# A two-layer transformer kernel: VectorE takes q's low part ahead of the two parts of the negated maxima

## The chip, the cores and the metric

The kernel runs on one core of one Trainium2 chip. The metric is the device time of one execution in microseconds (us), as the median of several runs. Engines are named as in the profile: PE is TensorE (its matrix multiplications; PEld its weight loads), DVE is VectorE, ACT is ScalarE, POOL is GpSimd, SP the queue that issues DMAs. L1232 is line 1232 of the kernel.

## The reference

The input x has 8 sequences of 512 rows of 128 values. Two layers follow one another, each an attention and a mixture of experts, with residuals:

```
x = x + cosine_attention(layernorm(x))         # 16 heads of 8, q and k normalized
x = x + top1_experts(layernorm(x))             # 8 experts, 128 -> 32 -> 128, gelu
x = x + causal_attention(layernorm(x))         # 16 heads of 64, softmax
x = layernorm(x + top2_experts(layernorm(x)))  # 8 experts, 128 -> 512 -> 128, gelu
```

The change touches the causal attention of the second layer. For each sequence and head it computes `a = q @ k.T / 8`, sets what lies above the diagonal to minus infinity, takes the softmax over the keys, multiplies by v, and projects all heads to 128 values. All is float32.

## The kernel before, in words

The 16 heads of the causal attention are taken in pairs, 8 pairs to a sequence, 64 in all. The main loop (`early_steps`) makes passes `i` over sequences and in each pass 8 steps `p` (0 to 7), one for each pair; every engine has its own program of the same loop, and semaphores alone connect them. The passes of this text are numbered by `i`; those from 0 to 7 have the causal attention of sequence `i`. A step works on several stages at once: scores and exponentials of pair g, the row maxima of pair g+1, the projections q and k of pair g+2, and the values of pair g-1. Beside them it carries a share of the work of other sequences: cosine attention (two batches of exponentials a step), layer norms, small experts, routing. After the passes comes the sparse second mixture of experts.

**High and low parts.** A projection lands in PSUM. ACT casts it to the matrix format fp32r (the high part, L941). DVE then subtracts the high part from the PSUM value (the low part, `lo_part`, L1209). The score is a sum of three products of such parts. The subtraction frees the PSUM bank that the projection lies in, and it waits for ACT's cast (`qk1_hi`). It occurs twice in a step, for q and for k.

**The maxima.** PE first computes scores from high parts alone (L1679), in three units to a pair. DVE adds the causal mask to them and reduces each row to its negated maximum (L1216, `maxima`). Then `maxima_parts` splits the 128x8 values into two bfloat16 parts with two operations on SBUF:

```
unit_done(dve, "max", g, 1)
unit_done(dve, "max", g, 2)
link(v.tensor_tensor(hl[:, :, :, 0], neg_max[:], neg_max[:], ALU.max))          # L1232
v.tensor_tensor(hl[:, :, :, 1], neg_max[:], hl[:, :, :, 0],
                ALU.subtract).then_inc(negmax_ready, 1)                         # L1233
```

`link` makes DVE wait until the first has completed. PE transposes the parts (L1690, `max_transposed`, the item "mT"), ACT moves them to SBUF, and the final scores of the next step take them in by a fourth product.

**What sets the order.** Each engine executes its program strictly in the order written. Two PSUM banks named `work` take all small results in turn; `work_order` lists the items of a step, and neighbours in that list lie in different banks, so that an item can be written only when the one two places before has been moved away. Around the change the list reads: q, one item that depends on the step, the row sums of pair g-1 ("sum", L1740 and L1742), mT, k. The item in between is a value projection in step 0, the transposed rows xtT, xh2T or xnT in steps 1 to 3, router logits in step 4 and the fourth q/k/v projection of the cosine attention in step 5; steps 6 and 7 have none, and in other steps it is missing where the sequence that it belongs to doesn't exist (the first and the last passes). PE's program has the same order: project q, the item, sums, mT, values of the cosine attention (L1856), project k, cosine scores (L1843).

**POOL's part.** When the sums are through PE, POOL may overwrite their operands: three additions over SBUF, one behind the other (L795 on 768 values a partition, L798 on 512, L801 on 256), each linked to the one before by a semaphore.

**DVE behind the change.** After q's low part DVE has, by step: the move of xh2T (step 2), of router logits (4), eight subtractions that split the operands of the cosine attention (L1251; steps 1, 3, 5, 7), four standardizations (L1185, step 5); then in every step the normalization by the inverse row sums (L1240), k's low part, and moves of transposed operands (L1262) that PE makes (L1829) when L1251 is done.

Of the kernel before, what the change touches and what calls it, by code (L numbers as in the profile page):

```python
# [281 lines left out]
def layers_kernel(nc, x, wqkv0, g_scale, wg0, s0, bias_ln0, w1_0, b1_0, w2_0, b2_0,  # L282
# [3 lines left out]
    with ctx:  # L286
# [280 lines left out]
        def work_bank(*name):  # L567
            return work[:, WORK_NO[name] % 2, :]
# [9 lines left out]
        def work_wait(eng, *name):  # L578

            eng.wait_ge(work_full[WORK_NO[name] % 2], work_fills(*name))  # L580
            return work_bank(*name)
# [8 lines left out]
        def free_of(*name):  # L590
            return work_free[WORK_NO[name] % 2]
# [15 lines left out]
        def unit_done(eng, *unit):  # L607
            eng.wait_ge(score_free[UNIT_NO[unit] % 2], unit_fills(*unit) + 1)
# [514 lines left out]
        def _(dve):  # L1123
# [3 lines left out]
            def link(ins):  # L1127

                links[0] += 1
                ins.then_inc(dve_step, 1)  # L1130
                dve.wait_ge(dve_step, links[0])
# [73 lines left out]
            def lo_part(which, hi, lo, g, n):  # L1205

                w = work_bank(which, g)
                dve.wait_ge(qk1_hi, n)
                v.tensor_tensor(lo[:, g % 2, :], w, hi[:, g % 2, :].bitcast(F32),  # L1209
                                ALU.subtract).then_inc(free_of(which, g), 1)  # L1210
# [8 lines left out]
            def maxima(g, i):  # L1219

                d = unit_wait(dve, "max", g, i)
                for j in range(2):
                    for qt, at in (((3, 0),), ((2, 0), (0, 3 * P)), ((1, 0),))[i]:
                        last = masked_max(d, qt, at, j)
                last.then_inc(unit_free("max", g, i), 1)

            def maxima_parts(g):

                unit_done(dve, "max", g, 1)
                unit_done(dve, "max", g, 2)  # L1230
                hl = neg_max_hl[:].rearrange("p t (j n) -> p t j n", j=2)
# [3 lines that stand above are left out]
# [192 lines left out]
            for o in early_steps():  # L1427
# [36 lines left out]
                    group_rows(s, p // 2 - 1)  # L1464
                if o.pair(1) is not None:
                    maxima(o.pair(1), 2)
                    maxima_parts(o.pair(1))
                if o.pair(2) is not None:
                    lo_part("q", q_hi, q_lo, o.pair(2), 2 * o.pair(2) + 1)
                if p == 2 and f is not None:  # L1470
                    w = work_wait(dve, "xh2T", f)
                    v.tensor_copy(xT_a, w).then_inc(free_of("xh2T", f), 1)
# [660 lines left out]
```

## Time and profile before

| | us |
|---|---|
| median of three runs | 1599.74 |
| lowest and highest | 1593.32, 1600.54 |
| the profiled execution | 1609.85 |
| its span on the core | 1608.1 |
| DVE busy | 979.8 (61%) |
| ACT busy | 863.5 (54%) |
| POOL busy | 605.1 (38%) |

Durations of single instructions come from the profiled execution, so sums are made against its time. A row of a timeline gives start, duration, engine, line and operation, the tiles written and read, their shapes and a count of merged instructions; what stands in square brackets is how long the engine had been idle before it and which instruction ended that. The granted clock of TensorE has two levels here, 1.00 (2.4 GHz) and 0.50 (1.2 GHz).

### The profile page before, as it was taken

What the parts mean: (1) busy time and instruction counts of PE and PEld (TensorE: products, weight loads), DVE (VectorE), ACT (ScalarE), POOL (GpSimd) and SP (SyncE); (2) the same over time, 40 slices, a digit from 0 to 9 for tenths busy, and PEclk for the clock granted to TensorE, in tenths of its full rate; (3) what the DMA queues carried; (4) which work ended last, traced back from release to release, by engine and by line L of the source; (5) the groups of instructions that cost most, each with busy time, mean ns of one, the idle gap of its engine ahead of it and who ended that gap; (6) DMA issues with size and microseconds to landing.
All of it is one profiled execution on the core that took longest, in us unless ns stands there. A gap on an engine that the chain in (4) does not pass through costs nothing.

```text
span 1608.1 us, 28398 instructions
## 1 busy us (share of the span) xinstructions
PE 1348.8 (84%) x9302; PEld 815.7 (51%) x9302; DVE 979.8 (61%) x3308; ACT 863.5 (54%) x1679; POOL 605.1 (38%) x783
## 2 busy tenths in 40 slices
PE   4778888889888888888888888989888987889873
PEld 1234444454545444544554545545555545778762
DVE  3565565656676666666666766565565653656664
ACT  4765555556555655565556555645433543455543
POOL 1000332233243324332433243325345445566564
PEclk7878899999999999999999999999899998999986
DMA  8050990000000000000000000001002001132412
GB/s 306 1 232 1 9 3 1 0 8 8 1 13 9 8 1 14 8 8 1 14 8 8 1 14 1 8 1 37 31 8 79 1 8 36 51 107 60 116 54 86
DMA packets 65455, 54.67 MB, mean 34 GB/s; under 512 B 41017, under 2 KB 51649, under 8 KB 65057
## 3 DMA queue, kind: packets, MB, share of 16 engines
q1 hardware_dynamic: 60768, 43.48, 12.6%
q0 software_dynamic: 4544, 9.38, 1.8%
q8 instruction: 79, 1.29, 0.3%
q14 instruction: 64, 0.52, 0.1%
HBM read 21.03 MB, written 31.81 MB: 33 GB/s over the span
## 4 chain that ended last, share of the span: by engine, by line
PE 62%; DVE 22%; ACT 11%; issue 3%; POOL 1%; DMA 0%; another core or an unknown queue 0%; SPq 0%; ACTq 0%; POOLq 0%; DVEq 0%
PE scores L1710 10%; PE work L1650 8%; PE outs L1856 7%; PE outs L1729 7%; DVE scores L1216 6%; ACT a_buf L935 6%; PE work L1759 4%; PE outs L2051 4%; PE scores L1679 4%; DVE ra L1209 3%; ACT ra L941 3%; DVE parts L1251 2%; PE scores L1843 2%; PE scores L2039 2%; PE work L1742 2%
## 5 line engine op out<-in xcount | busy, mean ns | idle before, releaser
L1216 DVE CUSTOM_DVE_ANT_0 scores<-scores,mask_qk 128x512 f32<-128x512 f32 (+3 forms) x512 | 239.1, 519 | 203.3 <-PE scores L1679 196.8
L785 POOL TENSOR_SCALAR_AFFINE_SELECT big<-big 128x256 f32<-128x256 f32 x256 | 101.6, 409 | 560.7 <-ACT big L929 560.4
L935 ACT ACTIVATE a_buf<-scores 128x1024 f32<-128x1024 f32 x256 | 248.2, 1028 | 104.7 <-PE scores L1843 104.4
L929 ACT ACTIVATE big<-scores 128x1024 f32<-128x1024 f32 (+1 forms) x192 | 169.4, 883 | 208.3 <-PE scores L1710 201.6
L1710 PE MATMUL scores<-ra 64*128 64x512 f32 (+3 forms) x1536 | 187.9, 350 | 37.6 <-ACT a_buf L935 24.3
L795 POOL TENSOR_TENSOR big<-big 128x768 f32<-128x768 f32 x64 | 117.0, 1828 | 151.3 <-PE work L1742 151.1
L1710 PEld LDWEIGHTS scores<-ra 64*128 64x128 f32 x1536 | 123.4, 191 | 88.2 <-ACT big L929 29.5
L1729 PE MATMUL outs<-big 128*64 128x512 f32 (+3 forms) x1024 | 162.4, 446 | 2.2 <-DVE yT L1240 2.2
L1856 PE MATMUL outs<-a_buf 128*16 128x512 f32 x1024 | 147.0, 650 | 1.5 <-ACT a_buf L935 1.4
L1090 ACT ACTIVATE big<-scores,b_sb 128x128 f32<-128x128 f32 x312 | 89.6, 371 | 83.3 <-PE scores L2039 46.9
L941 ACT CAST ra<-work 128x512 fp32r<-128x512 f32 x128 | 75.1, 586 | 96.5 <-PE work L1650 95.5
L1240 DVE TENSOR_TENSOR yT<-outs,rsum 128x512 f32<-128x512 f32 x64 | 44.1, 689 | 125.2 <-ACT rsum L952 125.2
L881 POOL DMA_INDIRECT choice_rows<-big x78 | 79.3, 1017 | 90.6 <-DVE big L1568 86.2
L1729 PEld LDWEIGHTS outs<-big 128*64 128x64 f32 x1024 | 64.6, 137 | 91.3 <-issue 78.1
L1209 DVE TENSOR_TENSOR ra<-work,ra 128x512 fp32r<-128x512 f32 x128 | 88.1, 689 | 33.5 <-ACT ra L941 28.4
L778 POOL TENSOR_TENSOR rstd<-var_eps,minus_half 128x4 f32<-128x4 f32 x48 | 50.2, 1046 | 149.4 <-DVE var_eps L1178 149.3
L1679 PE MATMUL scores<-ra 64*128 64x512 f32 (+3 forms) x512 | 82.8, 358 | 23.5 <-DVE neg_max L1216 20.0
L2051 PE MATMUL outs<-a_buf,big 128*128 x624 | 88.7, 288 | 8.2 <-ACT big L1090 3.7
L1843 PE MATMUL scores<-qkT 32*128 32x512 f32 x512 | 78.3, 515 | 17.6 <-ACT a_buf L935 12.6
L2051 PEld LDWEIGHTS outs<-a_buf,big 128*128 128x128 f32 x624 | 81.3, 203 | 9.9 <-issue 9.8
L1710 PE MATMUL scores<-neg_max_T,pick 64*128 64x512 f32 (+3 forms) x512 | 85.4, 328 | 0.0
L798 POOL TENSOR_TENSOR big<-big 128x512 f32<-128x512 f32 x64 | 82.4, 1287 | 5.0
(223 smaller groups left out, 2630.5 us busy)
## 6 DMA issues: line engine op xcount, KB each, us to landing
sorted_rows<-xrows SPq DMA_DIRECT2D x34, 520.0 KB, 6.7
big<-sorted_rows SPq DMA_DIRECT2D x78, 65.0 KB
a_buf<-in_w SPq DMA_DIRECT2D x2, 2048.0 KB, 8.2
a_buf<-in_x SPq DMA_DIRECT2D x8, 256.0 KB, 2.7
x_rows<-x SPq DMA_DIRECT2D x8, 256.0 KB, 2.0
ra<-x_rows SPq DMA_DIRECT2D x8, 256.0 KB
a_buf<-choice_rows SPq DMA_DIRECT2D x6, 256.0 KB, 3.8
yT<-choice_rows SPq DMA_DIRECT2D x5, 256.0 KB, 2.8
```

Of the source, the lines that this page charges most:

```text
L795: nc.gpsimd.tensor_tensor(tsum, prob1(g, 0)[:, :, P:SEQ], prob1(g, 1)[:, :, 0:3 * P], ALU.add).then_inc(tsum_step, 1)
L929: activation(prob1(g, i), d[:, :, 0:256] if i == 2 else d, ACT.Exp, scale=SCALE1).then_inc(unit_free("pair", g, i), 1)
L935: activation(prob0(c)[:, i * 1024:(i + 1) * 1024], unit_wait(act, "cosine", c, i), ACT.Exp).then_inc(unit_free("cosine", c, i), 1)
L941: copy(dst[:, g % 2, :], w).then_inc(qk1_hi, 1)
L1209: v.tensor_tensor(lo[:, g % 2, :], w, hi[:, g % 2, :].bitcast(F32), ALU.subtract).then_inc(free_of(which, g), 1)
L1216: return v.tensor_tensor_reduce(scores_, scores_, mask_qk[:, SEQ - width:SEQ], -1.0, 3e38, ALU.add, ALU.min, neg_max[:, qt, j:j + 1])
L1650: last = mm(dst, a, c, start=(n == 0), stop=(n == 2))
L1679: last = mm(d[:, j * SEQ + at:j * SEQ + at + width], q_hi[heads(j), g % 2, qt * P:(qt + 1) * P], k_hi[heads(j), g % 2, 0:width], start=(n ...
L1710: last = mm(d[:, j * SEQ + at:j * SEQ + at + width], lhs, c[heads(j), g % 2, queries], start=(n == 0 and term == 0), stop=(n == len(blocks ...
L1729: last = mm(outs[heads(j), 0, kb * P:], v1[:, kb, n * D1:(n + 1) * D1], probs, start=(kb == 0), stop=(kb == TILES - 1))
L1856: last = mm(outs[STRIP * j:STRIP * j + VCOLS, 1, :], vstat(s)[:, kb, g * HG + j, :], prob0(c)[:, j * SEQ:(j + 1) * SEQ], start=(kb == 0), ...
L2051: last = mm(y_bank, hid_T(n)[:, c * P:(c + 1) * P], w2_1_sb[:, bass.ds(expert[n] + c * P, DIM)], start=(c == 0), stop=(c == CH1 - 1))
```

## The change

In DVE's program of the main loop the call of `maxima_parts` goes behind that of `lo_part` for q. Both keep their conditions, and nothing else is altered.

```
@@ -1464,9 +1464,10 @@
                     group_rows(s, p // 2 - 1)
                 if o.pair(1) is not None:
                     maxima(o.pair(1), 2)
-                    maxima_parts(o.pair(1))
                 if o.pair(2) is not None:
                     lo_part("q", q_hi, q_lo, o.pair(2), 2 * o.pair(2) + 1)
+                if o.pair(1) is not None:
+                    maxima_parts(o.pair(1))
                 if p == 2 and f is not None:
                     w = work_wait(dve, "xh2T", f)
                     v.tensor_copy(xT_a, w).then_inc(free_of("xh2T", f), 1)
```

## Rows read from the trace of the kernel before

**Rows 1.** The page, parts 1 and 4: busy time, and the chain that ended last.
```profile
PE 1348.8 (84%) x9302; PEld 815.7 (51%) x9302; DVE 979.8 (61%) x3308; ACT 863.5 (54%) x1679; POOL 605.1 (38%) x783
PE 62%; DVE 22%; ACT 11%; issue 3%; POOL 1%; DMA 0%; another core or an unknown queue 0%; SPq 0%; ACTq 0%; POOLq 0%; DVEq 0%
```

**Rows 2.** List of waits: who waited for whom, us in total, times, longest.
```profile
PEld work L1740 <- DVE ra L1209: 44.0, 40, 1.4
...
PE work L1690 <- DVE ra L1209: 12.1, 20, 3.0
```

**Rows 3.** Timeline of an ordinary step (pass 4, step 0): start us, us, what.
```profile
805.23 0.59 ACT L941 CAST ra<-work 128x512 fp32r<-128x512 f32 x1 [0.83 <-PE work L1650]
...
805.55 0.20 DVE L1233 TENSOR_TENSOR neg_max_hl<-neg_max,neg_max_hl 128x8 bf16<-128x8 f32 x1
805.85 0.69 DVE L1209 TENSOR_TENSOR ra<-work,ra 128x512 fp32r<-128x512 f32 x1
...
807.61 0.40 PE L1690 MATMUL work<-ident_b,neg_max_hl 128*128 128x128 bf16 x4
...
807.77 1.83 POOL L795 TENSOR_TENSOR big<-big 128x768 f32<-128x768 f32 x1 [2.90 <-PE work L1742]
```

**Rows 4.** Timeline of a free step (pass 3, step 6).
```profile
767.98 0.20 DVE L1233 TENSOR_TENSOR neg_max_hl<-neg_max,neg_max_hl 128x8 bf16<-128x8 f32 x1
768.27 0.69 DVE L1209 TENSOR_TENSOR ra<-work,ra 128x512 fp32r<-128x512 f32 x1
...
768.73 1.82 POOL L795 TENSOR_TENSOR big<-big 128x768 f32<-128x768 f32 x1 [1.44 <-PE work L1742]
...
769.11 0.38 PE L1690 MATMUL work<-ident_b,neg_max_hl 128*128 128x128 bf16 x4 [0.48 <-DVE ra L1209]
...
770.63 1.28 POOL L798 TENSOR_TENSOR big<-big 128x512 f32<-128x512 f32 x1
```

**Rows 5.** Timeline of the first full step (pass 0, step 0).
```profile
169.33 1.82 POOL L795 TENSOR_TENSOR big<-big 128x768 f32<-128x768 f32 x1
...
169.69 1.52 DVE L1232 TENSOR_TENSOR neg_max_hl<-neg_max 128x8 bf16<-128x8 f32 x1
...
171.23 1.26 POOL L798 TENSOR_TENSOR big<-big 128x512 f32<-128x512 f32 x1
171.24 1.30 DVE L1233 TENSOR_TENSOR neg_max_hl<-neg_max,neg_max_hl 128x8 bf16<-128x8 f32 x1
...
173.27 0.38 PE L1690 MATMUL work<-ident_b,neg_max_hl 128*128 128x128 bf16 x4 [3.02 <-DVE ra L1209]
```

**Rows 6.** Instructions on the tile neg_max_hl: duration ns min/median/max, first and last start.
```profile
L1232 DVE TENSOR_TENSOR neg_max_hl<-neg_max x64: 194/196/1518, 153.3 to 1328.0; 128x8 bf16<-128x8 f32 x64
L1233 DVE TENSOR_TENSOR neg_max_hl<-neg_max,neg_max_hl x64: 194/196/1717, 153.5 to 1328.2; 128x8 bf16<-128x8 f32 x64
```

**Rows 7.** Timeline of a free step with operand parts (pass 3, step 7).
```profile
790.47 0.59 ACT L941 CAST ra<-work 128x512 fp32r<-128x512 f32 x1 [0.76 <-PE work L1650]
...
792.38 0.55 PE L1829 MATMUL work<-ident_r,parts 128*128 128x128 f32 x4 [1.51 <-DVE parts L1251]
...
793.58 0.54 PE L1829 MATMUL work<-ident_r,parts 128*128 128x128 f32 x4 [0.65 <-DVE ra L1209]
```

**Rows 8.** Timeline of an ordinary step (pass 4, step 5).
```profile
904.70 4.32 DVE L1185 TENSOR_SCALAR a_buf<-res,mean,rstd 128x128 f32<-128x128 f32 x4
...
910.27 0.53 PE L1829 MATMUL work<-ident_r,parts 128*128 128x128 f32 x4 [2.32 <-DVE ra L1209]
```

**Rows 9.** Two stretches (PE, PEld, DVE, ACT, POOL, granted clock), then L1650 at either clock.
```profile
911.40:914.80 3.40, 3.36 (x18) 1.90 (x20) 1.27 (x4) 1.36 (x2) 0.00 (x0) 0.50 0.03 7
785.00:795.00 10.00, 7.21 (x54) 3.80 (x52) 9.19 (x23) 6.32 (x14) 7.00 (x8) 1.00 0.04 13
...
L1650 PE MATMUL work<-x_lo,wqkv_hi 128*128 128x512 f32 x1 | 0.6, 628 | 0.0
...
L1650 PE MATMUL work<-x_hi,wqkv_lo 128*128 128x512 f32 x6 | 2.4, 394 | 0.0
```

More of the change, by code:

```diff
@@ L1466, in _ @@
                     maxima(o.pair(1), 2)
-                    maxima_parts(o.pair(1))
                 if o.pair(2) is not None:
                     lo_part("q", q_hi, q_lo, o.pair(2), 2 * o.pair(2) + 1)
+                if o.pair(1) is not None:
+                    maxima_parts(o.pair(1))
                 if p == 2 and f is not None:
```

## The prediction

> **What bounds the kernel now.** I read the page first: TensorE (PE) is busy 84% of the span and carries 62% of the chain that ended last, VectorE (DVE) 22% [rows 1]. A microsecond that PE idles is therefore mostly a microsecond of time; one that DVE idles is not. The list of waits comes next, for where PE waits for the two operations exchanged. It waits for q's low part (L1209) ahead of the row sums (L1740) 40 times, and ahead of the transposition of the maxima (L1690, "mT") 20 times [rows 2]. The timelines of single steps show why there are two kinds.
>
> In an *ordinary* step something stands between q and the sums in the bank order, so the sums need the bank that q's low part frees. ScalarE's cast of q ends at 805.82; the parts of the maxima (L1232, L1233) are done by 805.75; the low part runs 805.85 to 806.54; the sums follow, mT starts at 807.61, and GpSimd's long addition (L795) at 807.77 [rows 3].
>
> In a *free* step q, sum, mT follow one another in the bank order. The sums don't wait, mT shares q's bank. The parts end at 768.18, the low part at 768.96, mT starts at 769.11 after PE idled 0.48 us; and GpSimd's addition has been running since 768.73, before the low part is done [rows 4]. Steps 6 and 7 of all seven passes that have them in full are of this kind, and five more at the edges where the item in between is missing (steps 3 and 4 of the first, 5 of pass 5, 1 and 2 of pass 7): 19. This fits the row of 20 waits that sum to 12.1 us: 19 of 0.48 us and one of 3.02 [rows 2, 4, 5].
>
> **The change part by part.** Nothing is added or removed, and no DMA is in the moved stretch: 64 pairs of two small DVE operations of about 0.2 us each [rows 6] go behind a 0.69 us subtraction, and the two waits for the maxima's score slots go with them (already met, since q's cast ends later). The moved pair takes 0.20 + 0.03 + 0.20 = 0.43 us, with the wait of the second part for the first (171.21 to 171.24 in rows 5).
>
> *The low part of q earlier: worth nothing.* It starts 0.03 us behind the cast's end, not behind the parts [rows 3]. In both kinds of step the cast is the later one, by 0.1 us or more; in some steps 7 by 0.0. I take 0; the most it could give is in the rivals.
>
> *The parts later, ordinary steps.* They will end about 0.45 us behind the low part, at 807.0 in the step of rows 3, and mT can't start before the sums are through, at 807.61. 0.6 us of cover, price 0. GpSimd starts 1.2 us behind the low part and misses them. If the sums did not cover it, 0.45 us each.
>
> *The parts later, free steps: this is the sum's main term.* Here they would start at 768.9 in the step of rows 4, 0.2 us after GpSimd's addition. The trace has that meeting once: in the first full step GpSimd starts L795 at 169.33, DVE starts L1232 at 169.69, and this operation on 8 elements per partition takes 1.52 us instead of 0.2, to 171.21, just behind the end of L795. L1233 then starts 171.24, L798 171.23, and it too is held, 1.30 us, until L798 ends [rows 5]. In the last step L1233 alone meets L795 and takes 1.72 us; these are the only long ones among 128 (medians 0.20, maxima 1.52 and 1.72) [rows 6]. So both parts will be held, one behind L795, one behind L798. With GpSimd at its present times L798 ends at 771.91, the second part 0.05 later, mT starts at about 772.03 instead of 769.11: +2.92 us.
>
> The Trainium skill ("SBUF — State Buffer", Who interferes with whom) says that a VectorE instruction with both inputs in SBUF contends with a GpSimd instruction that reads SBUF, and that the one issued first keeps the shared port for its whole length while the other blocks. By that rule, the trace agrees (1.52 us in rows 5); but its second half, "issue order", is also what could let the second part slip through, which is rival B.
>
> How much of 2.92 us stays, step by step:
> - 12 steps in full (seven steps 6, the steps 7 of passes 5 and 6, step 4 of the first pass, steps 1 and 2 of pass 7). PE runs on behind mT without a pause worth naming, and ScalarE and DVE hang on k's projection behind it. 12 x 2.92 = 35.0.
> - 6 steps (the steps 7 of passes 0 to 4, step 3 of the first) have slack: PE waits 1.51 us for the operand parts (L1829 at 792.38) and 0.65 for k's low part (at 793.58). k's cast, now at 790.47, goes to 793.4 and ends 0.59 later, k's low part 0.7 behind, at 794.7; the transposes at 793.58 go to 794.75 [rows 7]. 6 x 1.17 = 7.0.
> - Step 5 of pass 5 has still more slack: 0.7 taken, between 0 and 1.2.
>
> *DVE later by the pair in step 5 of passes 0 to 4.* Behind the low part stand eight subtractions, then four standardizations of which the first just gets by GpSimd and the others are held (4.32 us for four) [rows 8]. PE waits 2.32 us for k's low part behind them. Pushed 0.4 us, one more of these operations falls behind L795. I take 0.5 us each, 2.5; bounds 0 and 2.0 each.
>
> In steps 1 and 3 the subtractions' tail may be caught too, but the sum's inverse that the next DVE operation waits for comes later: 0, at most 0.3. The first two steps: the first has nothing hiding the pair (+0.6), the second has both parts held already and will do the low part meanwhile (-0.7): 0 together.
>
> *The clock.* In the free steps PE's idle time grows from 0.48 to 3.4 us. After an idle 2.32 us in front of L1829 at 910.27 the granted clock was 0.50 (1.2 GHz) over 911.4 to 914.8 [rows 8, 9]. A matmul of 128x512 takes 628 ns at 1.2 GHz, 394 at 2.4 [rows 9], so PE loses up to 0.37 of such a stretch, 3.4 x 0.37 = 1.3 us. Three of the 19 steps are followed by a 1.2 GHz stretch already; 16 x 1.3 = 20.8. Bounds: 0 (no new stretch), and 19 x 2.6 = 49 where each lasts twice as long; the value is that of rows 8 and 9, the nearest in length.
>
> Sum: 35.0 + 7.0 + 0.7 + 2.5 + 20.8 = **+66 us**. The profiled execution took 1609.85 us (span 1608.1): 1676. It lies 10.1 us above the median of the three runs, 1599.74; on the median's footing I predict **1666 us**.
>
> **The rivals.**
> - B, *the second part slips past.* Only 0.01 us lie between the starts of L798 and L1233 in rows 5. If L1233 wins, mT is held 1.64 us (to the end of L795 at 770.55, plus 0.2): 12 x 1.64 = 20, the six steps with slack about 0.3 each, 2.5 for step 5, 21 for the clock, as 2.1 us of idle remain: +45, **1645**. For it: the closeness. Against: the one case went the other way, and both engines' gaps are fixed ones.
> - C, *held, but the clock stays up*: +45, **1645**. For it: the idle 1.51 us of rows 7 has no stretch at 1.2 GHz behind it (granted 1.00 over 785 to 795 [rows 9]), and 3.4 us at other places may differ. Against: rows 8 and 9, in which a stretch followed 2.32 us.
> - D, *the parts are not held*, because DVE comes straight from the subtraction: 12 x 0.45 + 7 x 0.4 + 5 x 0.4 = +10, **1610**. Against: rows 5, in which nothing but GpSimd's running addition held them.
> - E, *the bank comes free sooner* (the other side). If DVE rather than the cast set the start of the low part, PE's 40 waits ahead of the sums [rows 2] would shorten by 0.43 us each: 17 us, **1583**. It decides where the cast ends before the maxima do; in rows 3 and 4 it ends half a microsecond after them.
> - F, *no change*: ordinary steps alone counting, **1600**. It would need the free steps to have changed kind.
>
> **How the numbers follow.** A 0.62, B 0.15, C 0.12, D 0.05, E 0.02, F 0.04. A, B, C and D are all slower by more than 0.5% (8 us, about what a measurement here can tell from no change): 0.94; same 0.04; faster 0.02. A's own range is 1648 to 1694 by the bounds of the clock; B and C lie at its lower end, and with step 5 at nothing they reach 1635. Range 1635 to 1692.
>
> **What would show it.** After the change L1232 and L1233 have medians of 0.2 us still, but 19 or so each of about 1.7 and 1.3 us. The waits of L1690 for L1233 grow to some 19 of 3.4 us; the waits ahead of L1740 stay as they are, 40 of 0.7 to 1.1. q's low part starts 0.03 us behind the cast as before. There are some 16 more stretches with the granted clock at 0.5. Wrong would be: L1233 at 0.2 us in free steps (B), few new stretches (C), neither held (D), a shorter wait ahead of L1740 (E).

## The result, and the profile after

The changed kernel takes **1666.62 us** (median of 4 runs, 1664.46 to 1671.59) against 1598.28 us before (4 runs, 1593.32 to 1600.54). The ratio is 1.0436, with a 95% interval of 1.0401 to 1.0471. The prediction said 1666 us, range 1635 to 1692.

The profiled span went from 1608.1 to 1664.9 us. I split it at the first score matmul of the first pair and at that of the last; what lies between is called *the loop* below, and a step runs from its first score matmul to that of the next. The loop went from 1175.9 to 1240.2 us (+64.3), what lies ahead of it from 159.7 to 159.2, and what lies behind it from 272.5 to 265.5, in which nothing was changed. So the two profiled executions differ by 56.8 us and the medians by 68.3. In the runs below the part ahead of the loop is sometimes 159 to 162 and sometimes 170 us, whatever the kernel; therefore experiments are compared by their loops as well as by their times.

The loop of the kernel before is known from one execution, and it was a long one: 1609.85 us, where the median is 1598.28. It had 16.8 us at 1.2 GHz in three early steps (0 and 1 of pass 0, 0 of pass 1), where ten of the eleven other traces of this text have 0 to 7.4. That is chance and not the kernel: e3 and e9, which are one kernel, have 15.8 and 3.4 there. A usual loop before is therefore probably some us shorter than 1175.9. Steps in which neither trace has low clock don't suffer from this, and the argument rests on them where it can.

The page after, parts 1 and 4, which answer to [rows 1]:

```profile
PE 1363.0 (82%) x9302; PEld 820.3 (49%) x9302; DVE 1007.7 (61%) x3308; ACT 863.8 (52%) x1679; POOL 603.2 (36%) x783
...
PE 58%; DVE 21%; ACT 11%; issue 6%; POOL 2%; POOLq 1%; DMA 1%; SPq 0%; ACTq 0%; DVEq 0%
```

PE is busy longer in the loop though it does the same work (1028.1 us, now 1049.7). On the chain that ended last GpSimd's share went from 1% to 2%, and "issue" from 3% to 6%. The list of waits after (PE's lines stand one further down, L1691 for L1690), beside [rows 2]:

```profile
PE work L1691 <- DVE neg_max_hl L1233: 66.3, 21, 3.4
...
PEld work L1741 <- DVE ra L1209: 44.4, 40, 1.4
```

The wait ahead of the transposition of the maxima was 12.1 us for the low part; it is 66.3 us for the second part of the maxima. That ahead of the sums stands where it stood (44.0, now 44.4 us).

The timeline of the step of [rows 4] in the changed kernel (pass 3, step 6):

```profile
790.33 0.59 ACT L941 CAST ra<-work 128x512 fp32r<-128x512 f32 x1 [0.84 <-PE work L1651]
...
790.95 0.69 DVE L1209 TENSOR_TENSOR ra<-work,ra 128x512 fp32r<-128x512 f32 x1 [0.63 <-ACT ra L941]
...
791.41 1.80 POOL L795 TENSOR_TENSOR big<-big 128x768 f32<-128x768 f32 x1 [1.44 <-PE work L1743]
791.56 1.71 DVE L1232 TENSOR_TENSOR neg_max_hl<-neg_max 128x8 bf16<-128x8 f32 x1
793.29 1.26 POOL L798 TENSOR_TENSOR big<-big 128x512 f32<-128x512 f32 x1
793.30 1.30 DVE L1233 TENSOR_TENSOR neg_max_hl<-neg_max,neg_max_hl 128x8 bf16<-128x8 f32 x1
...
794.66 0.61 PE L1691 MATMUL work<-ident_b,neg_max_hl 128*128 128x128 bf16 x4 [3.35 <-DVE neg_max_hl L1233]
```

Read it downward: the low part starts 0.03 us behind the cast, as before; 0.46 us later GpSimd starts; 0.15 us behind it L1232 starts and ends just after GpSimd does; L1233 loses to the next addition by 0.01 us; PE has been idle for 3.35 us, where it was 0.48. L1232 took over 0.6 us in 18 steps (1 before, the first step), L1233 in 20 (2 before, the first and the last). In 18 of these, all free steps, both are held, and in each L1233 started 6 to 11 ns behind L798.

An ordinary step (the one of [rows 3], pass 4, step 0) is untouched; mT follows the sums without an idle moment, and GpSimd comes later:

```profile
837.26 0.40 PE L1691 MATMUL work<-ident_b,neg_max_hl 128*128 128x128 bf16 x4
837.43 1.84 POOL L795 TENSOR_TENSOR big<-big 128x768 f32<-128x768 f32 x1 [2.91 <-PE work L1743]
```

In pass 4, steps 0 to 7 changed by 0.03, 0.02, -0.01, -0.12, 0.00, 0.25, 4.29 and 2.67 us. It is all in steps 5, 6 and 7. Over the whole loop the 18 free steps with held parts grew by 68.1 us together, with 71.6 us more at 1.2 GHz; the other seven steps 5 grew by 3.0 us; the remaining 38 steps became 6.9 us shorter, with 17.7 us less at 1.2 GHz.

### The profile page after: what moved, and what is told of

Read it like the earlier page. It is cut to its first block, busy times and chain, and to the rows that moved or that the text cites. A ratio compares the mean times of both kernels' runs of the same rounds, so it can differ in the third digit from the quotient of the medians.

```text
span 1664.9 us, 28398 instructions
## 1 busy us (share of the span) xinstructions
PE 1363.0 (82%) x9302; PEld 820.3 (49%) x9302; DVE 1007.7 (61%) x3308; ACT 863.8 (52%) x1679; POOL 603.2 (36%) x783
## 4 chain that ended last, share of the span: by engine, by line
PE 58%; DVE 21%; ACT 11%; issue 6%; POOL 2%; POOLq 1%; DMA 1%; SPq 0%; ACTq 0%; DVEq 0%
PE scores L1711 9%; PE work L1651 9%; PE outs L1857 7%; PE outs L1730 7%; ACT a_buf L935 5%; DVE scores L1216 5%; PE work L1760 4%; PE scores L1680 4%; ACT ra L941 3%; DVE ra L1209 3%; PE outs L2052 2%; PE scores L1844 2%; DVE neg_max_hl L1232 2%; DVE a_buf L1185 2%; DVE neg_max_hl L1233 2%
## 5 line engine op out<-in xcount | busy, mean ns | idle before, releaser
L795 POOL TENSOR_TENSOR big<-big 128x768 f32<-128x768 f32 x64 | 116.8, 1825 | 149.5 <-PE work L1743 149.3
L1857 PE MATMUL outs<-a_buf 128*16 128x512 f32 x1024 | 154.7, 680 | 2.0 <-ACT a_buf L935 2.0
L1209 DVE TENSOR_TENSOR ra<-work,ra 128x512 fp32r<-128x512 f32 x128 | 88.3, 690 | 87.2 <-ACT ra L941 86.9
L941 ACT CAST ra<-work 128x512 fp32r<-128x512 f32 x128 | 75.1, 586 | 113.2 <-PE work L1651 112.1
L1240 DVE TENSOR_TENSOR yT<-outs,rsum 128x512 f32<-128x512 f32 x64 | 44.2, 690 | 113.2 <-ACT rsum L952 112.9
L1844 PE MATMUL scores<-qkT 32*128 32x512 f32 x512 | 79.4, 525 | 17.3 <-ACT a_buf L935 12.3
L798 POOL TENSOR_TENSOR big<-big 128x512 f32<-128x512 f32 x64 | 81.8, 1278 | 5.0
```

The costliest lines, as they stand in the source:

```text
L795: nc.gpsimd.tensor_tensor(tsum, prob1(g, 0)[:, :, P:SEQ], prob1(g, 1)[:, :, 0:3 * P], ALU.add).then_inc(tsum_step, 1)
L941: copy(dst[:, g % 2, :], w).then_inc(qk1_hi, 1)
L1857: last = mm(outs[STRIP * j:STRIP * j + VCOLS, 1, :], vstat(s)[:, kb, g * HG + j, :], prob0(c)[:, j * SEQ:(j + 1) * SEQ], start=(kb == 0), ...
```

## The experiments

Theory H: a DVE instruction that reads SBUF twice waits for a GpSimd addition that is already running, and the change puts the pair there. Theory C: the rest is TensorE's clock after the longer idle time. The time at 1.2 GHz inside the loop is summed from the trace's records of the granted clock. Times are medians; e9 and e10 and the runs beside them are single. The third column is the kernel before on the same chip. A loop and its time at 1.2 GHz come from one profiled execution, which can lie far from the median: 9 us above it in e4, 10 below in e7, 9 below in e8. The kernel of e3 and e9 gave two loops 9.7 us apart, so a change of the loop below 10 us says little by itself.

| kernel | time, us | before beside it | loop | change of loop | at 1.2 GHz in loop |
|---|---|---|---|---|---|
| before | | | 1175.9 | | 93.0 |
| changed | 1666.6 | 1598.3 | 1240.2 | +64.3 | 150.5 |
| e1 GpSimd waits | 1614.1 | 1597.4 | 1183.4 | +7.5 | 105.8 |
| e2 free steps old | 1618.5 | 1597.4 | 1181.3 | +5.4 | 109.2 |
| e3 step 6 alone | 1660.5 | 1597.4 | 1237.0 | +61.1 | 208.2 |
| e4 PE filled | 1647.1 | 1597.4 | 1218.9 | +43.0 | 95.6 |
| e5 second part only | 1637.0 | 1603.6 | 1201.0 | +25.1 | 113.2 |
| e6 one input | 1649.6 | 1603.6 | 1213.6 | +37.7 | 150.2 |
| e7 GpSimd after DVE | 1582.5 | 1603.6 | 1140.9 | -35.0 | 64.9 |
| e8 step 6, PE filled | 1639.7 | 1603.6 | 1196.4 | +20.5 | 103.3 |
| e9 = e3 again | 1662.3 | 1611.4 | 1227.3 | +51.4 | 177.5 |
| e10 step 7 alone | 1619.6 | 1611.4 | 1193.2 | +17.3 | 123.6 |

**e1, GpSimd waits for the parts.** The order of the change stays.

```
                 if g:
                     work_wait(pool, "sum", g - 1)
+                pool.wait_ge(negmax_ready, min(g + 2, ALL_PAIRS))
```

> The changed kernel, with one wait more: GpSimd starts its first addition (L795) only when the two parts of the negated maxima of the step are done. Theory H (the parts are held by GpSimd's additions): both parts take 0.2 us in every step except the first; the transposition of the maxima starts about 0.45 us later than in the kernel before instead of 2.92 in the 12 free steps without slack (5 us), and the operand subtractions, which now meet an addition that starts 0.7 us later, cost about 0.7 us in 6 steps (4 us); with step 5 about +10 us on the kernel before, 1608 us, and no new stretches at 1.2 GHz. Rival R (the place behind the subtraction itself costs, by a PSUM bank or by DVE's queue, whatever GpSimd does): 1667 us as in the changed kernel, with the parts at 0.2 us and the waits of L1690 unchanged.

The ratio to before is 1.010 (1.003 to 1.017), against 1.044 for the change. The instructions on the tile of the parts (ns min/median/max):

```profile
L1233 DVE TENSOR_TENSOR neg_max_hl<-neg_max x64: 182/184/196, 164.8 to 1348.9; 128x8 bf16<-128x8 f32 x64
L1234 DVE TENSOR_TENSOR neg_max_hl<-neg_max,neg_max_hl x64: 195/196/197, 165.0 to 1349.2; 128x8 bf16<-128x8 f32 x64
```

Neither part is ever long, not even in the first and last step, and PE's wait for the second part, 66.3 us in the changed kernel, is 17.8. PE idles 0.72 us ahead of mT in a free step. The place behind the subtraction is cheap by itself: free steps without low clock in either trace grew by 0.24 to 0.36 us (expected 0.45 in those without slack), ordinary ones by almost nothing. The loop is 7.5 us longer. What I had wrong is the clock: I expected no new stretches, and there are 12.8 us more at 1.2 GHz. The time of 1614 instead of 1608 also contains a part ahead of the loop of 170 us. Rival R is out.

**e2, the old order in the free steps alone** (those in which "sum" stands directly behind "q" in `work_order`).

```
                     maxima(o.pair(1), 2)
+                    if free_step(o):
+                        maxima_parts(o.pair(1))
                 if o.pair(2) is not None:
                     lo_part("q", q_hi, q_lo, o.pair(2), 2 * o.pair(2) + 1)
-                if o.pair(1) is not None:
+                if o.pair(1) is not None and not free_step(o):
                     maxima_parts(o.pair(1))
```

> The changed kernel, with the old order in the free steps (those in which the row sums stand directly behind q in the bank order) and the new one in all others, 44 of 63. Theory H: back to the kernel before, 1598 us, at most 2 us above for step 5 of passes 0 to 4 (0.25 us each); neither part is ever held but in the first and the last step. Rival R (the delay of 0.43 us on DVE costs in every step): some 44 x 0.4 = 18 us above, 1616 us.

The time is a miss: 1618.5 us, ratio 1.0135 (1.006 to 1.021). The loop tells the parts of it apart. It is 5.4 us longer. In steps 0 to 4 and 6 to 7 nothing changed by more than 0.12 us, and nearly always by less than 0.03, wherever neither run had a stretch at 1.2 GHz (rival R wanted 0.4 in each with the new order), and step 5 of pass 4 took 0.27 us more. What there is beside is 16 us more at 1.2 GHz, and 10 us ahead of the loop. So the other steps are innocent, but the time by itself would not have shown it; why the clock was low for longer here stays open.

**e3, the new order in step 6 alone** (7 of 64 steps; the condition of e2 is `not (o.p == 6 and 0 <= o.i <= 6)`).

> The kernel before, with the new order in step 6 of passes 0 to 6 alone (7 steps of 64). Theory H: each such step pays 2.9 us for the held parts and about 1.4 us for a stretch at 1.2 GHz, 7 x 4.3 = +30 us, 1628 us, with L1232 at 1.7 us and L1233 at 1.3 us seven times. Without the clock's part it would be 7 x 2.9 = +20 us, 1618 us. Rival R (64 x the average cost of the change, 1.06 us): 7 x 1.06 = +7 us, 1606 us.

Also a miss, upward: 1660 us instead of 1628. Seven held pairs cost nearly as much as eighteen. Step 6 of pass 4 grew from 20.33 to 25.91 us, and steps that nothing touches grew too (step 0 by 2.62, step 3 by 0.75, step 4 by 1.34), each where the clock was low for longer. The mean granted clock over the whole loop was 0.92; before it was 0.96. What remained open was whether this is chance, and whether it is the clock at all: e9 and e8.

**e4, PE kept busy while the parts are held.** The change, with idle matmuls ahead of the wait.

```
             def max_transposed(g):

+                o = Step((g - 1) // PAIRS, (g - 1) % PAIRS)
+                ...
+                    d = unit_open(pe, "cosine", o.cosine(1), 0)
+                    for _ in range(12):
+                        mm(d[:, 0:SEQ], wqkv1_hi[:, 0, 0:P], x2_hi[:], start=True, stop=True)
                 pe.wait_ge(negmax_ready, g + 1)
```

> The changed kernel, with 12 idle matmuls of 128x512 on PE ahead of the transposition of the maxima in the steps 6 and 7 of passes 0 to 5 and two other free steps, 14 in all; their results go to a scores slot that the next cosine scores overwrite, and they end (12 x 0.22 = 2.6 us) before the held parts do. Theory C (the time beyond the 2.92 us of holding is the clock, which falls after PE's idle 3.34 us): the idle time falls to about 0.7 us, the granted clock stays at 1.00 behind these steps, and 14 x 1.35 = 19 us come back: 1648 us, the parts held as before. Rival (the clock is not what costs): 1667 us or, if the fillers are in the way, more.

Measured 1647.1 us. The timeline of step 6, pass 4:

```profile
948.36 3.01 PE L1695 MATMUL scores<-x_hi,wqkv_hi 128*128 128x512 f32 x12
...
948.53 1.84 POOL L796 TENSOR_TENSOR big<-big 128x768 f32<-128x768 f32 x1 [1.44 <-PE work L1751]
948.68 1.75 DVE L1233 TENSOR_TENSOR neg_max_hl<-neg_max 128x8 bf16<-128x8 f32 x1
...
951.84 0.40 PE L1699 MATMUL work<-ident_b,neg_max_hl 128*128 128x128 bf16 x4 [0.46 <-DVE neg_max_hl L1234]
```

The parts are held as before (the second for 1.32 us) and mT comes as late, but PE idles only 0.46 us ahead of it. The time at 1.2 GHz in the loop falls from 150.5 to 95.6 us and the loop by 21.3. It was 180 useless matmuls in 15 steps (I had counted 14), and the kernel became 19 us faster. What is left of the loop's change, 43.0 us with 2.6 us more low clock than before, is nearly all the price of holding. A microsecond at 1.2 GHz costs 21.3 / 54.9 = 0.39 us by this pair; by e3 and e9, one kernel with two amounts of low clock, 9.7 / 30.7 = 0.32. Below I use 0.35, an estimate that can be off by a tenth.

**e5, only the second part behind the low part.** The first stays ahead.

```
                     maxima(o.pair(1), 2)
+                    maxima_parts(o.pair(1))      # L1232 alone
                 if o.pair(2) is not None:
                     lo_part("q", q_hi, q_lo, o.pair(2), 2 * o.pair(2) + 1)
                 if o.pair(1) is not None:
-                    maxima_parts(o.pair(1))
+                    second_part(o.pair(1))       # L1233 before
```

> The changed kernel with the first part (L1232) back ahead of q's low part; only the second part (L1233 before) goes behind it, in every step. This is the price of rival B by itself. Theory H: L1232 takes 0.2 us; the second part is held by the first addition alone and takes about 1.7 us in 18 or 19 steps, 0.2 in the others; PE's idle time ahead of L1690 there is 2.0 us instead of 3.34. Holding costs 12 x 1.5 = 18 us and little in the 6 steps with slack; the loop from the first score matmul to the last pair, 1175.9 us in the kernel before, becomes some 1196 us plus 0.35 us for each further us at 1.2 GHz. Time 1620 to 1640 us. Rival (what costs is the link between the two parts, not GpSimd): the second part takes 0.2 us, and the time is 1600 us.

1637.0 us. Less the clock (20.2 x 0.35 = 7.1), the loop is 18.0 us longer, where 12 x 1.5 was expected. Four free steps without slack have no low clock in either trace, and they show the 1.5 without any conversion: they grew by 1.52 to 1.55 us. That the sum fits so well is partly chance, since most ordinary steps grew by 0.04 to 0.10 us too, which I had at nothing. The step 6 of pass 4:

```profile
936.06 1.80 POOL L795 TENSOR_TENSOR big<-big 128x768 f32<-128x768 f32 x1 [1.44 <-PE work L1748]
936.28 1.63 DVE L1237 TENSOR_TENSOR neg_max_hl<-neg_max,neg_max_hl 128x8 bf16<-128x8 f32 x1
```

PE idles 2.01 us ahead of mT. No link to another DVE instruction is in play here; it is GpSimd's addition that holds it.

**e6, a first part that reads SBUF once.** The change, with one operation replaced.

```
-                link(v.tensor_tensor(hl[:, :, :, 0], neg_max[:], neg_max[:], ALU.max))
+                link(v.tensor_reduce(hl[:, :, :, 0], neg_max[:].unsqueeze(3), AX.X, ALU.max))
```

> The changed kernel with the first part computed by a tensor_reduce (a maximum over one element), which reads SBUF once, instead of a tensor_tensor that reads it twice; the second part stays as it is. Theory P (two SBUF inputs make an instruction wait for GpSimd's addition): the first part takes about 0.2 us though the addition is running, the second alone is held, 1.5 us; PE's idle time ahead of L1690 is about 2.0 us and the time that of e5_second_only. Rival (every DVE instruction that reads SBUF is held): both are held, 1.7 and 1.3 us, idle time 3.34 us, time 1667 us as in the changed kernel.

Step 6 of pass 4:

```profile
947.64 1.80 POOL L795 TENSOR_TENSOR big<-big 128x768 f32<-128x768 f32 x1 [1.42 <-PE work L1743]
947.79 0.18 DVE L1232 TENSOR_REDUCE neg_max_hl<-neg_max 128x8 bf16<-128x8 f32 x1
948.00 1.49 DVE L1233 TENSOR_TENSOR neg_max_hl<-neg_max,neg_max_hl 128x8 bf16<-128x8 f32 x1
...
949.55 0.40 PE L1691 MATMUL work<-ident_b,neg_max_hl 128*128 128x128 bf16 x4 [2.00 <-DVE neg_max_hl L1233]
```

Inside the running addition the reduction takes 0.18 us (never over 0.19 in 64), where the instruction with two inputs took 1.71. The idle time is that of e5, 2.0 us, and the loop less the clock (57.2 x 0.35 = 20.0) is 17.7 us longer against 18.0; the three free steps without slack and without low clock grew by 1.52 to 1.55 us, as in e5. The time is a miss, 1649.6 us instead of e5's: the clock again. The Trainium skill ("SBUF — State Buffer", Who interferes with whom) names this difference, between one SBUF input and two, and lets `tensor_reduce` never contend on trn2; by that rule, this run agrees. The run changes the kind of the instruction together with the number of its inputs, so it doesn't say which of the two matters; e7 bears on that.

**e7, the held instructions of the kernel before.** The steps of [rows 7 and 8] have DVE instructions held as well: four standardizations take 4.32 us (L1185), and in step 7 of pass 3 eight subtractions 4.38 (L1251). The old order, with GpSimd behind DVE in two kinds of step:

```
                 causal(g, 2, 0)
+                o = Step(g // PAIRS, g % PAIRS)
+                if o.p == 7 and o.h is not None:
+                    pool.wait_ge(parts_ready, o.h * GROUPS0 + 1)
+                if o.p == 5 and o.f is not None:
+                    pool.wait_ge(rows_ready["f0"], o.f * 3 + 3)
```

> The kernel before (old order) with one wait more on GpSimd: in step 7 of passes 0 to 4 it starts its additions after DVE's eight operand subtractions (L1251), in step 5 after DVE's four standardizations (L1185). Theory H says that holding costs in the kernel before too: in step 7 the subtractions take 1.2 us instead of 4.4 and PE's idle 1.51 us ahead of L1829 is gone, in step 5 the standardizations take 1.1 us instead of 4.3 and of PE's idle 2.32 us about 0.4 stay. Loop 5 x 1.8 + 6 x 1.9 = 20 us shorter than 1175.9 and some 10 us more by a clock that doesn't fall in step 5: time 1570 us. Rival (GpSimd's own delay of 1 to 2 us comes back later, or something else is late in the same place): 1598 us.

It is faster than both kernels: ratio 0.987 (0.982 to 0.992), 21 us by the medians. The time, 1582.5, is 12 us above what I wrote, beside a kernel before that ran at 1603.6 there. The loop, 35.0 us shorter, flatters it: the profiled execution was the fastest of six (1572.8), and 3.9 us of the 35.0 lie in steps 0 and 1 of pass 0, ahead of all that the edit touches. In step 5 of pass 4:

```profile
876.99 1.11 DVE L1190 TENSOR_SCALAR a_buf<-res,mean,rstd 128x128 f32<-128x128 f32 x4
...
878.18 1.83 POOL L800 TENSOR_TENSOR big<-big 128x768 f32<-128x768 f32 x1 [3.57 <-DVE a_buf L1190]
...
880.74 0.54 PE L1834 MATMUL work<-ident_r,parts 128*128 128x128 f32 x4 [0.50 <-DVE ra L1214]
```

The four standardizations take 1.11 us instead of 4.32, PE idles 0.50 instead of 2.32 [rows 8], and step 5 is 1.82 us shorter, step 7 1.76. GpSimd's delay of a microsecond comes back nowhere: steps without low clock in either trace agree within 0.05 us. The clock answers too: steps 5 and 6 of passes 0 to 4 had 3.4 to 6.8 us at 1.2 GHz in each pass, and here they have none.

One by one, the four standardizations take 0.34, 1.90, 1.44 and 0.88 us in the kernel before, so the last three are held; each takes 0.34 here. Each reads one SBUF tensor and, as scalars, a column of means and one of inverse deviations. So the line doesn't run simply between one SBUF tensor and two: a `tensor_scalar` with one tensor was held, and the `tensor_reduce` of e6 was not. No run here separates the kind of instruction from the number and shape of its inputs.

**e8, step 6 alone with PE filled** (e3 with the matmuls of e4 in step 6).

> The new order in step 6 alone as in e3_step6_new, with 12 idle matmuls ahead of the transposition of the maxima in step 6 of passes 0 to 5. In e3_step6_new the loop became 61 us longer, 20 of them by holding (7 x 2.9), and the time at 1.2 GHz in it rose from 93 to 208 us. Theory C (the rest, 41 us, is the clock, which falls after the idle 3.34 us and, once the steps have shifted, at other idle places too): with PE kept busy there, the time at 1.2 GHz in the loop returns to about 100 us and the loop to 1176 + 20 = 1196 us, the time to about 1620 us. Rival (the new order in step 6 alone makes something else late): loop about 1237 us as in e3_step6_new, time 1660 us.

The loop is 1196.4 us and the time at 1.2 GHz in it 103.3: both as theory C has it. Against e3 that is 40.6 us of loop for 104.9 us less at 1.2 GHz. But the two profiled executions are extremes, that of e3 the longest of four and that of e8 the shortest: by the medians, each against its kernel before, e3 cost 63 us and e8 36, and the filling gave back 27. The direction is the clock's, and the 41 us are more than a usual pair of executions shows. The time, 1639.7 as the median, is above the 1620 expected.

This run also has what the changed kernel never showed. In step 6 of pass 6 the first part was held, 1.70 us, and the second was not:

```profile
1237.05 1.33 POOL L799 TENSOR_TENSOR big<-big 128x512 f32<-128x512 f32 x1
1237.05 0.19 DVE L1239 TENSOR_TENSOR neg_max_hl<-neg_max,neg_max_hl 128x8 bf16<-128x8 f32 x1
```

The second part started 6 ns behind the addition and ran through beside it, and the addition took 1.33 us instead of 1.26. The step, without low clock in either trace, grew by 1.76 us instead of 2.9. In step 0 of pass 0 the same happened here and in e7. In all traces of this text together the second part started 5 to 12 ns behind the middle addition 74 times; it was held 71 times and slipped past 3 times, each time at 6 ns, a distance at which it was held in other steps.

**e9, e3 once more.**

> The kernel of e3_step6_new once more, for whether its 208 us at 1.2 GHz inside the loop belong to the kernel. If they do (the same idle places at the same distances let the clock fall in each pass), the loop is again 1230 to 1240 us and the time at 1.2 GHz 195 to 220 us, with low stretches in steps 6, 0, 3 and 4 of passes 1 to 5; if they are chance, the loop lies anywhere between 1200 and 1240 us.

Loop 1227.3, low clock 177.5 us: both under the ranges I gave for a pattern that is wholly the kernel's. From pass 3 to 5 the steps do agree with e3 within 0.15 us (step 6 of pass 4: 25.91 and 25.92), low stretches included; the first three passes differ. So part of it repeats and part is chance.

**e10, step 7 alone.**

> The kernel before, with the new order in step 7 of passes 0 to 6 alone. Theory H: both parts held in these 7 steps (1.7 and 1.3 us), and of the 2.92 us a step passes 0 to 4 keep 1.2 each, passes 5 and 6 all: 5 x 1.2 + 2 x 2.9 = 12 us of loop by holding; and 0.35 us for every us by which the time at 1.2 GHz in the loop exceeds 93 us. Loop 1188 us if it doesn't. Rival (the slack in step 7 absorbs nothing): 7 x 2.9 = 20 us, loop 1196 us.

17.3 us, of which 30.6 x 0.35 = 10.7 for the clock, leaves 6.6 for holding instead of 12. Some of the difference is in the first pass, where steps 0 to 6 were 5.7 us faster than in the profile before, by their clock; the steps 7 of passes 1 to 4 were 2.0 to 2.5 us longer with 3.4 to 4.1 us of low clock, which leaves 0.7 to 1.3 for holding where I expected 1.2. Over the seven steps 7 alone, the holding reckoned in this way is 10.9 us.

## Why the prediction was right

- *The low part earlier: nothing.* Right. It starts 0.03 us behind the cast in both kernels, and the waits ahead of the sums did not move. DVE now idles there instead: ahead of L1209 it waits for the cast 86.9 us in 107 waits, where it was 28.4 in 47. What was taken out ahead of the low part had been filling a wait.
- *The parts in ordinary steps: covered.* Right: without low clock in either trace the ordinary steps other than step 5 changed by 0.12 us at most, in the changed kernel and in e2.
- *The parts in free steps: both held, +2.92 us.* Right. Step 7 of pass 5, in which neither kernel has low clock, grew by 2.88 us. I had counted 19 such steps; it was 18. Step 3 of the first pass escaped, because the sums ran at 1.2 GHz there: the second part ended at 227.88, and L795 started at 228.12.
- *The six steps with slack: 1.17 us each.* Right for the steps 7: in e4, where they have no low clock, they grew by 1.20 to 1.21 us in passes 1 to 4. The sixth was step 3 of the first pass, which escaped.
- *Step 5: 0.5 us each.* It was 0.25 (0.17 to 0.39); the sum is small.
- *The clock: +20.8 us.* Loop +57.5 us at 1.2 GHz, x 0.35 = 20.1 (18 to 22 with 0.32 to 0.39; I had priced it at 0.37), and 33 stretches where there were 19. That longer idle time brings low clock is right, and e4 confirms it. That the size came out so near is luck. In the free steps themselves the clock cost 71.6 x 0.35 = 25 us, and 6 came back in steps in which the profile before happened to be low for longer; the steps 7 of passes 5 and 6 had no low clock at all; and e3 shows 115 us more at 1.2 GHz, 40 us of time, with fewer held steps. I had tied one stretch to each idle place. e3 and e9 show low stretches in steps that nothing touches, so the place of later idle times seems to matter as well; no run isolates that, and I had no row for it.
- *The sum.* Predicted 45.2 for holding and DVE, measured 64.3 - 20.1 = 44.2 in the loop. For the profiled execution I had 1676 us, and it took 1666.6: +57 instead of +66. Most of the difference is the 7.0 us gained behind the loop, which are in no step of mine. The medians agree within 1 us (1666 and 1666.62, +68.3) only because I had taken off the 10.1 us by which the profiled execution before exceeded its median. The sum was sound to within some 10 us; the last digit is luck.
- *The range.* Its ends don't follow from the terms. With the clock at 0 the sum gives 1645, not 1648, and with step 5 at nothing about 1642, not 1635; the upper end was 1694, and I wrote 1692. The measured time is nowhere near either end.

The rivals: B (the second part slips past) did not occur in the changed kernel; L798 won in all 18 free steps, by 6 to 11 ns. I had called the gaps of both engines fixed and given B 0.15. It does occur, 3 times in 74 meetings (e7, e8), and what decides it isn't shown. Its price is measured by e5, 18.0 us of holding, where I had 20. C is refuted by the 57.5 us more at 1.2 GHz and by e4, D by both parts held in 18 steps and by e1, E by the unmoved wait ahead of the sums, F by the result.

## What to carry to other kernels

Before you move a short instruction of VectorE by half a microsecond, look at what GpSimd runs at the new place, not only at what the instruction waits for: two operations on 8 elements took 3.0 us here instead of 0.4. Such holding stands in a profile as busy time and not as a wait, so compare an instruction's longest time with its median (1.71 and 0.2 us here). Count the places where an instruction does nothing but fill a wait; taking it out of there gains nothing. And where two versions differ by PE's idle times, compare the granted clock before believing a difference of one or two per cent: the same held pair cost 2.9 us in a step without low clock and up to 7.5 in one with 11 us of it (step 6 of pass 6 in e3 and e9).

## What the runs showed that I had not expected

- The clock's share isn't proportional to the cause. With 7 held steps the loop was 61.1 us longer (208 us at 1.2 GHz), with 18 it was 64.3 (150 us). From pass 3 to 5 the pattern repeats from pass to pass and in the second run (e3, e9); its cause stays open.
- Useless matmuls paid: 19 us in e4, and in e8 against e3 27 us by the medians, 41 by the loops.
- The kernel before paid for holding in two kinds of step, and a wait on GpSimd there gave back 21 us by the medians (35 by the loops).
- A `tensor_reduce` of 0.18 us with one SBUF input passes a running addition. A `tensor_tensor` with two doesn't, and neither does the `tensor_scalar` with one tensor and two scalar columns.
- Who wins a meeting at 6 ns isn't settled: the second part slipped past the addition in 3 of 74.
